# Turning the sums of an attention chunk with a 66-column fp32 product instead of 128-column transposes

## The chip, the cores and the metric

The kernel runs on one core of a Trainium2 chip. The metric is the device time of one execution in microseconds (us). The kernel before takes 3548.26 us, the median of 3 runs (3547.71 to 3548.54).

## What is computed

Two layers in sequence: differential attention over 2048 tokens of width 512 with 16 pairs of heads, a mixture of experts, a state-space layer and a quantised feed-forward layer, with a layer norm after each. The change lies in the attention alone:

```python
q = (x @ Wq).reshape(b, t, 2 * H, HD).transpose(0, 2, 1, 3) * scaling     # H = 16, HD = 16
k = (x @ Wk).reshape(b, t, 2 * H, HD).transpose(0, 2, 1, 3)
v = (x @ Wv).reshape(b, t, H, 2 * HD).transpose(0, 2, 1, 3)
scores = jnp.einsum('bhqd,bhkd->bhqk', q, k)
aw = jax.nn.softmax((scores + causal).astype(jnp.float32), axis=-1)
aw = aw.reshape(b, H, 2, t, t)
aw = aw[:, :, 0] - lam * aw[:, :, 1]
attn = jnp.einsum('bhqk,bhkd->bhqd', aw, v)
```

So each pair of heads has two softmaxes over the same keys, whose results are subtracted, and then multiplies with a V of 32 columns.

## The kernel before

The function `attention` works on 16 pairs (`p`), and in each on 4 chunks of 512 queries (`c`). A chunk has 4c + 4 key tiles of 128 keys, since later keys are hidden; one key tile of one chunk is a unit `u`, and a pair has 40. Scores are made turned, with keys on the partitions and queries along the row.

TensorE runs one program written out by hand (from L601). In each unit it does, in this order: `scores` for the unit two ahead (L560), products for the row maxima of a later pair (`max_scores`, L552), and `times_v` for this unit (L583). `times_v` multiplies the exponentials `PT` with `VS`, which holds V's 32 columns, a column of ones that gives the softmax's denominator, and zeros up to 64. The two softmaxes of a pair lie on partitions 0 to 63 and 64 to 127 of the sums `po`, so of its 128 rows 2 x 33 have a meaning: 0 to 32 and 64 to 96. Both products of a unit are full fp32.

At the end of a chunk ScalarE copies `po` to `OT` (L662). One unit later, after that unit's `times_v`, TensorE turns the copy with `turn_out` (L587 to L593): four transposes of 128x128, each giving 128 queries on the partitions and the 128 sums along the row. They fill one bank of PSUM, a slot of a ring of three that the products for the maxima use as well. VectorE's `combine` (L700 to L714) reads the slot: the reciprocals of the two denominators, their weights, two products with the 32 columns of each softmax, and the sum into `A`. It empties the slot with the last of these reads.

VectorE also takes the row maxima out of the ring (L681, L684), in the order in which TensorE fills it. Before TensorE writes a slot it waits until the tenant of three fillings ago is out (`await_ring`). ScalarE makes the exponentials (L628), copies the sums, and rounds weights for a later layer. GpSimd fills VS, stages V for each pair (L464), hides later keys in the diagonal units (L482), and takes the low parts of those weights. SyncE waits for the fills (L513) before it loads the third pair's queries and keys.

`g.ident` is the 128x128 identity in fp32, made at the start of the program.

Of the kernel before, what the change touches and what calls it, by code (L numbers as in the profile page):

```python
# [14 lines left out]
P = 128  # L15
# [12 lines left out]
VD = 2 * HD  # L28
# [318 lines left out]
def attention(nc, g, QD, KD, scan_w, next_w):  # L347
# [10 lines left out]
    MV = 64  # L358
# [58 lines left out]
    with ExitStack() as ctx:  # L417
        sb = lambda name, shape, dt=F32: ctx.enter_context(nc.sbuf_tensor(name, shape, dt))
# [4 lines left out]
        OT = [sb(f"outT{b}", [P, CHUNK]) for b in range(2)]  # L423
# [2 lines left out]
        mp = sb("neg_max_parts", [P, P], F32R)  # L426
        mT = sb("neg_max_turned", [P, P], F32R)
        rL = sb("inv_sums", [P, 4, 2])
        r2 = sb("weight2", [P, 4])
        o1, o2 = sb("out1", [P, 4, VD]), sb("out2", [P, 4, VD])  # L430
        w_raw = sb("w_raw", [P, 2, E])
# [4 lines left out]
        ring = [ctx.enter_context(nc.psum_tensor(f"ring{i}", [P, CHUNK], F32)) for i in range(RING)]  # L436
        pb = [ctx.enter_context(nc.psum_tensor(f"prob_scores{i}", [P, 2, CHUNK], F32)) for i in range(2)]
        po = ctx.enter_context(nc.psum_tensor("times_v", [P, CHUNK], F32))
        setup, mp_clear = g.sem("at_setup"), g.sem("max_parts_clear")
        loaded, max_in = [[g.sem(f"{n}{b}") for b in range(NQK)] for n in ("at_loaded", "at_max_in")]  # L440
        filled, emptied = g.sem("ring_filled"), g.sem("ring_emptied")
        max_all, max_high, max_low = (g.sem("max_" + n) for n in ("all", "high", "low"))
# [16 lines left out]
        with nc.Block() as block:  # L459

            @block.gpsimd
            def _(pool):
                def stage_v(p):
                    pool.tensor_copy(VS[p % 2][:, :, 0:VD], g.V[:, :, p * VD:(p + 1) * VD]).then_inc(v_staged, 1)  # L464

                for b in range(2):
                    pool.memset(VS[b][:, :, :], 0.0).then_inc(setup, 1)
                pool.wait_ge(setup, 2)
                for b in range(2):
                    pool.memset(VS[b][:, :, VD], 1.0).then_inc(setup, 1)  # L470
                stage_v(0)
                for b in range(2, NQK):
                    pool.memset(KS[b][:, :].bitcast(F32), 1.0).then_inc(setup, 1)
                pool.memset(mp[:, :].bitcast(F32), 0.0).then_inc(mp_clear, 1)
                for p in range(PAIRS):

                    if p:
                        stage_v(p)
                    for u in diag:
                        pool.wait_ge(exped, p * NU + u + 1)  # L480
                        keys = PT[u % NPT][:, :, 0:P]
                        pool.affine_select(out=keys, in_=keys, compare_op=ALU.is_ge, fill=0.0, base=0,  # L482
                                           pattern=[[0, 2], [1, P]], channel_multiplier=-1).then_inc(hidden, 1)
                        for n in range(by_unit.get(u, 0)):
                            k = len(SPLIT_AT) * p + n + (by_unit[11] if u > 11 else 0)
                            pool.wait_ge(w_high, k + 1)
                            if k >= 2:
                                pool.wait_ge(w_out[k % 2], 32 * (k // 2))
                            pool.tensor_tensor(w_lo[:, k % 2, :], w_raw[:, k % 2, :], w_hi[:, k % 2, :].bitcast(F32), ALU.subtract).then_inc(w_low, 1)  # L489
                        if p == PAIRS - 1 and u == ends[NCH - 2]:  # L490
                            for n in range(len(UP_AT)):
                                pool.wait_ge(up_high, n + 1)
                                pool.tensor_tensor(up_lo[:, piece(n)], g.raw_up[:, piece(n)], up_hi[:, piece(n)].bitcast(F32), ALU.subtract).then_inc(up_low, 1)
# [40 lines left out]
            @block.tensor  # L534
            def _(pe):
                def slot(n):
                    return ring[n % RING]

                def await_ring(n):

                    if n >= RING:
                        pe.wait_ge(emptied, n - RING + 1)

                def max_scores(q, t):
                    i, c = tiles[t]
                    w = tile_width(t)
                    if t == 0 and q > 1:
                        pe.wait_ge(loaded[q % NQK], loads(q))
                    await_ring(place["max", q, t, 1])
                    for s in range(2):  # L550
                        rows = slice(64 * s, 64 * s + PARTS)
                        pe.matmul(slot(place["max", q, t, s])[:, 0:w], QS[q % NQK][rows, i * P:(i + 1) * P],  # L552
                                  KS[q % NQK][rows, c * CHUNK:c * CHUNK + w], start=True, stop=True).then_inc(filled, 1)

                def scores(b, u):
                    c, j = units[u]
                    w = width(u)
                    for s in range(2):
                        rows = slice(64 * s, 64 * s + FULL)
                        mm = pe.matmul(pb[u % 2][:, s, 0:w], KS[b][rows, j * P:(j + 1) * P],  # L560
                                       QS[b][rows, (c + 1) * CHUNK - w:(c + 1) * CHUNK], start=True, stop=True)
                    mm.then_inc(scored, 1)

                def times_v(p, u):

                    c, j = units[u]
                    w = width(u)
                    if u in diag:
                        pe.wait_ge(hidden, p * ND + diag.index(u) + 1)
                    else:  # L570
                        pe.wait_ge(exped, p * NU + u + 1)
                    if u == 0:
                        pe.wait_ge(v_staged, p + 1)
                        if p == 0:
                            pe.wait_ge(setup, 4)
                    if j == 0:
                        if p or c:
                            pe.wait_ge(po_free, p * NCH + c)
                    halves = 2 if w > 256 else 1
                    h = w // halves  # L580
                    for n in range(halves):
                        for s in range(2):
                            mm = pe.matmul(po[MV * s:MV * (s + 1), CHUNK - w + n * h:CHUNK - w + (n + 1) * h], VS[p % 2][:, j, :],  # L583
                                           PT[u % NPT][:, s, n * h:(n + 1) * h], start=(j == 0 and n == 0), stop=(j == 4 * c + 3))
                    mm.then_inc(pt_free, 1)

                def turn_out(p, c):  # L587
                    n = place["out", p, c]
                    await_ring(n)
                    pe.wait_ge(po_free, p * NCH + c + 1)  # L590
                    for k in range(4):
                        mm = pe.transpose(slot(n)[:, k * P:(k + 1) * P], OT[c % 2][:, k * P:(k + 1) * P], g.ident[:, :])
                    mm.then_inc(filled, 1)  # L593

                def turn_maxima(q):
                    n = place["turn", q]
                    await_ring(n)
                    pe.wait_ge(max_low, q)
                    pe.transpose(slot(n)[:, 0:P], mp[:, :].bitcast(F32), g.ident[:, :]).then_inc(filled, 1)

                for u in range(LEAD):  # L601
                    scores(0, u)
                for p in range(PAIRS):
                    for u in range(NU):
                        n = p * NU + u
                        to = p + (u + LEAD) // NU
                        if to < PAIRS:
                            if u + LEAD == NU:
                                pe.wait_ge(max_in[to % NQK], rows(to))

                            pe.wait_ge(exped, n + 1)
                            scores(to % NQK, (u + LEAD) % NU)
                        for q, t in step_tiles(p, u):
                            max_scores(q, t)
                        if u == TURN_AT and p + 1 < PAIRS:
                            turn_maxima(p + 1)
                        times_v(p, u)
                        if u == 0 and p:
                            turn_out(p - 1, NCH - 1)
                        if u - 1 in ends:  # L620
                            turn_out(p, ends.index(u - 1))
                turn_out(PAIRS - 1, NCH - 1)

            @block.scalar
# [42 lines left out]
            def _(dve):  # L667
                def slot(n):
                    return ring[n % RING]
# [30 lines left out]
                def combine(p, c):  # L700
                    n, m = place["out", p, c], p * NCH + c
                    dve.wait_ge(filled, n + 1)
                    tp = slot(n)[:, :].rearrange("p (k s n) -> p k s n", k=4, s=2)
                    dve.reciprocal(rL[:, :, :], tp[:, :, :, VD]).then_inc(out_inv, 1)
                    dve.wait_ge(out_inv, m + 1)
                    dve.tensor_scalar(r2[:, :], rL[:, :, 1], g.neg_lam[:, :], None, ALU.mult).then_inc(out_weight, 1)
# [1800 lines left out]
```

## Time and profile before

| | before |
|---|---|
| median of 3 runs | 3548.26 us |
| the profiled execution | 3550.99 us, with a span of 3549.0 us from its first to its last instruction |
| TensorE matmul / weight load busy | 3370.3 us (95%) / 2378.6 us (67%) |
| VectorE / ScalarE / GpSimd busy | 2677.5 (75%) / 2110.0 (59%) / 880.6 us (25%) |
| mean granted clock of TensorE | 0.977 |
| attention, first to last instruction | about 166 to 1223 us |

"Busy" of TensorE counts the time in which any matmul is in flight. Matmuls are pipelined, so one that takes 0.27 us from start to end may follow the last after 0.11 us; what a step costs is read from starts, not from durations. Weight loads are listed as an engine of their own (PEld) and overlap the multiplies. In a row, `128*64 128x256` says that the array holds 128 rows and 64 columns of weights and that 256 columns stream through. `ring<-ident,outT` means that tile ring is written from ident (which streams) and outT (which is loaded as weights).

### The profile page before, as it was taken

What the parts mean: (1) busy time and instruction counts of PE and PEld (TensorE: products, weight loads), DVE (VectorE), ACT (ScalarE), POOL (GpSimd) and SP (SyncE); (2) the same over time, 40 slices, a digit from 0 to 9 for tenths busy, and PEclk for the clock granted to TensorE, in tenths of its full rate; (3) what the DMA queues carried; (4) which work ended last, traced back from release to release, by engine and by line L of the source; (5) the groups of instructions that cost most, each with busy time, mean ns of one, the idle gap of its engine ahead of it and who ended that gap; (6) DMA issues with size and microseconds to landing.
All of it is one profiled execution on the core that took longest, in us unless ns stands there. A gap on an engine that the chain in (4) does not pass through costs nothing. (4 is left out here: it accounts for less than half of the span.)

```text
span 3549.0 us, 58273 instructions
## 1 busy us (share of the span) xinstructions
PE 3370.3 (95%) x20672; PEld 2378.6 (67%) x20672; DVE 2677.5 (75%) x5224; ACT 2110.0 (59%) x3378; POOL 880.6 (25%) x818
## 2 busy tenths in 40 slices
PE   9899999999999888977999999999999999969998
PEld 7644444444444477765777777777777777758886
DVE  3577777777777484575999999999998999964444
ACT  3156666666667633434777777777777777743332
POOL 0012212222222300002344434443444444420000
PEclk9999999999999998988999999999999999989999
DMA  7333433433432211237666766677667766640100
GB/s 243 84 79 90 113 86 100 110 88 100 108 90 86 101 39 35 86 113 243 235 225 230 245 233 227 231 254 243 228 227 231 247 228 231 216 141 27 36 12 24
DMA packets 263840, 529.34 MB, mean 149 GB/s; under 512 B 32256, under 2 KB 54912, under 8 KB 260480
## 3 DMA queue, kind: packets, MB, share of 16 engines
q1 hardware_dynamic: 263552, 525.62, 46.7%
q8 instruction: 166, 2.72, 0.3%
q14 instruction: 122, 1.00, 0.1%
HBM read 429.55 MB, written 95.42 MB: 148 GB/s over the span
## 5 line engine op out<-in xcount | busy, mean ns | idle before, releaser
L628 ACT ACTIVATE probs<-prob_scores 128x1024 f32<-128x1024 f32 (+3 forms) x640 | 572.8, 897 | 382.2 <-PE prob_scores L560 374.4
L583 PE MATMUL times_v<-probs,VS 128*64 128x256 f32 (+2 forms) x4608 | 613.5, 382 | 17.5 <-ACT outT L662 12.7
L684 DVE TENSOR_REDUCE part_max<-ring 128x1 f32<-128x512 f32 x720 | 463.0, 686 | 112.4 <-PE ring L552 110.7
L49 PE MATMUL sc_pip<-sc_xh,sc_wl 128*128 128x512 f32 x1024 | 455.7, 445 | 22.3 <-DMA sc_xl<-x_low 15.4
L583 PEld LDWEIGHTS times_v<-probs,VS 128*64 128x64 f32 x4608 | 279.8, 136 | 256.8 <-issue 161.8
L51 PE MATMUL sc_pip<-sc_xh,sc_wh 128*128 128x512 f32 x1024 | 405.2, 396 | 0.0
L50 PE MATMUL sc_pip<-sc_xl,sc_wh 128*128 128x512 f32 x1024 | 403.9, 394 | 0.0
L1754 POOL TENSOR_TENSOR sc_xdd<-sc_xdt,sc_small 128x512 f32<-128x512 f32 x128 | 245.6, 1919 | 581.5 <-DVE sc_xdt L1965 581.5
L1890 ACT ACTIVATE sc_M<-sc_later,sc_small 128x128 f32<-128x128 f32 x1024 | 311.8, 390 | 0.0
L560 PE MATMUL prob_scores<-QS,KS 50*128 50x512 f32 (+3 forms) x1280 | 298.8, 464 | 4.0 <-ACT probs L628 2.1
L1956 DVE SCALAR_TENSOR_TENSOR sc_ca<-sc_xr,sc_chan,sc_ca 128x512 f32<-128x512 f32 x384 | 290.9, 758 | 13.6
L560 PEld LDWEIGHTS prob_scores<-QS,KS 50*128 50x128 f32 x1280 | 119.4, 183 | 217.2 <-ACT probs L628 119.1
L681 DVE CUSTOM_DVE_ANT_0 masked_scores<-ring,later_keys 128x128 f32<-128x128 f32 x480 | 216.4, 488 | 59.0 <-PE ring L552 56.4
L49 PEld LDWEIGHTS sc_pip<-sc_xh,sc_wl 128*128 128x128 f32 x1024 | 194.1, 190 | 96.8 <-issue 40.5
L552 PE MATMUL ring<-KS,QS 48*128 48x512 f32 (+3 forms) x1200 | 233.9, 386 | 14.3 <-DVE part_max L684 12.5
L50 PEld LDWEIGHTS sc_pip<-sc_xl,sc_wh 128*128 128x128 f32 x1024 | 194.3, 190 | 68.1 <-issue 29.5
L1774 POOL TENSOR_TENSOR sc_ssq<-sc_ssq,sc_sq 128x512 f32<-128x512 f32 x112 | 163.3, 1458 | 307.2 <-ACT sc_sq L1918 307.2
L51 PEld LDWEIGHTS sc_pip<-sc_xh,sc_wh 128*128 128x128 f32 x1024 | 193.5, 189 | 43.7
L1805 PE MATMUL sc_py<-sc_M,sc_xdt 128*64 128x128 f32 x2048 | 207.4, 281 | 10.2 <-DVE sc_M L1976 10.2
L2002 DVE TENSOR_TENSOR sc_gl<-sc_gx,sc_gh 128x512 fp32r<-128x512 f32 x128 | 216.4, 1690 | 0.0
L482 POOL TENSOR_SCALAR_AFFINE_SELECT probs<-probs 128x256 f32<-128x256 f32 x256 | 104.5, 409 | 449.2 <-ACT probs L628 449.2
L489 POOL TENSOR_TENSOR w_lo<-w_raw,w_hi 128x512 fp32r<-128x512 f32 x96 | 122.6, 1278 | 359.1 <-ACT w_hi L641 359.1
(376 smaller groups left out, 7163.6 us busy)
## 6 DMA issues: line engine op xcount, KB each, us to landing
sc_wh<-scan_W_high SPq DMA_DIRECT2D x256, 256.0 KB, 2.8
sc_wl<-scan_W_low SPq DMA_DIRECT2D x256, 256.0 KB, 3.4
sc_later<-scan_acum SPq DMA_DIRECT2D x128, 512.0 KB, 4.9
sc_ce<-scan_expa SPq DMA_DIRECT2D x128, 512.0 KB, 5.2
sc_woh<-scan_Wo_high SPq DMA_DIRECT2D x128, 256.0 KB, 4.1
sc_wol<-scan_Wo_low SPq DMA_DIRECT2D x128, 256.0 KB, 4.8
w_raw<-in_Wg SPq DMA_DIRECT2D x64, 256.0 KB, 2.9
scan_W_high<-w_hi SPq DMA_DIRECT2D x64, 256.0 KB, 2.0
```

Source lines behind the costliest of these rows:

```text
L49: pe.matmul(out, ll, rh, start=start, stop=False)
L50: pe.matmul(out, lh, rl, start=False, stop=False)
L51: return pe.matmul(out, lh, rh, start=False, stop=stop)
L552: pe.matmul(slot(place["max", q, t, s])[:, 0:w], QS[q % NQK][rows, i * P:(i + 1) * P], KS[q % NQK][rows, c * CHUNK:c * CHUNK + w], start=T ...
L560: mm = pe.matmul(pb[u % 2][:, s, 0:w], KS[b][rows, j * P:(j + 1) * P], QS[b][rows, (c + 1) * CHUNK - w:(c + 1) * CHUNK], start=True, stop= ...
L583: mm = pe.matmul(po[MV * s:MV * (s + 1), CHUNK - w + n * h:CHUNK - w + (n + 1) * h], VS[p % 2][:, j, :], PT[u % NPT][:, s, n * h:(n + 1) * ...
L628: act.activation(PT[u % NPT][:, :, 0:w], pb[u % 2][:, :, 0:w], ACT.Exp).then_inc(exped, 1)
L681: dve.tensor_tensor_reduce(out=masked_out[:, s, 0:w], in0=slot(n)[:, 0:w], in1=later[:, CHUNK - w:], scale=1.0, scalar=NEG, op0=ALU.add, o ...
L684: dve.tensor_reduce(to, slot(n)[:, 0:w], AX.X, ALU.max).then_inc(emptied, 1)
L1754: pool.tensor_tensor(xdd[t % 2][:, :, :], xdt[t % 2][:, :, :], bc(t, 1), ALU.mult).then_inc(xdd_made, 1)
L1890: act.activation(M[t % 2][:, h, :], later[t % 2][:, h, :], ACT.Relu, bias=small[b % 2][:, c, 3, h:h + 1], scale=-1.0).then_inc(relued, 1)
L1956: dve.scalar_tensor_tensor(out=to, in0=src, scalar=w, in1=to, op0=ALU.mult, op1=ALU.add).then_inc(conv if last else conv_step, 1)
```

## The change

A constant matrix `pick` of 128 x 66 is made of two copies of 33 columns of the identity: columns 0 to 32 and 64 to 96. `turn_out` multiplies by it, as an ordinary product in fp32, in place of each transpose. The four results lie side by side in 264 columns of the slot, and `combine` reads them there with another stride. GpSimd makes `pick` right after the first staging of V, ahead of the fills of the third K buffer and of the parts of the maxima, and TensorE waits for it once, at the first turned chunk.

```diff
         rL = sb("inv_sums", [P, 4, 2])
+
+        pick = sb("pick", [P, 2, VD + 1])
...
-        setup, mp_clear = g.sem("at_setup"), g.sem("max_parts_clear")
+        setup, mp_clear, picked = g.sem("at_setup"), g.sem("max_parts_clear"), g.sem("picked")
+        NP = 2 * (VD + 1)
...
                 stage_v(0)
+                for s in range(2):
+                    pool.tensor_copy(pick[:, s, :], g.ident[:, MV * s:MV * s + VD + 1]).then_inc(picked, 1)
...
                     pe.wait_ge(po_free, p * NCH + c + 1)
+                    if p == 0 and c == 0:
+                        pe.wait_ge(picked, 2)
                     for k in range(4):
-                        mm = pe.transpose(slot(n)[:, k * P:(k + 1) * P], OT[c % 2][:, k * P:(k + 1) * P], g.ident[:, :])
+                        mm = pe.matmul(slot(n)[:, k * NP:(k + 1) * NP], OT[c % 2][:, k * P:(k + 1) * P], pick[:, :, :], start=True, stop=True)
                     mm.then_inc(filled, 1)
...
-                    tp = slot(n)[:, :].rearrange("p (k s n) -> p k s n", k=4, s=2)
+                    tp = slot(n)[:, 0:4 * NP].rearrange("p (k s n) -> p k s n", k=4, s=2)
```

## Rows read from the trace of the kernel before

**Rows 1.** One stretch of attention: busy us of each engine, granted clock, DMA.
```profile
core 0: us, PE busy (x) PEld busy (x) DVE busy (x) ACT busy (x) POOL busy (x), PEclk, DMA share, GB/s
350.00:525.00 175.00, 171.21 (x1247) 85.33 (x1243) 135.22 (x369) 108.00 (x134) 39.96 (x63) 1.00 0.42 101
```

**Rows 2.** What TensorE waited for in attention: us in total, times, longest us.
```profile
PE times_v L583 <- ACT outT L662: 12.7, 47, 0.9
PE ring L552 <- DVE part_max L684: 12.5, 35, 0.8
PE times_v L583 <- POOL probs L482: 3.6, 2, 2.6
PE prob_scores L560 <- ACT probs L628: 1.2, 1, 1.2
PE ring L592 <- ACT outT L662: 0.8, 1, 0.8
```

**Rows 3.** The replaced line: duration min/median/max; then who waited for it.
```profile
L592 PEld LDWEIGHTS ring<-ident,outT x256: 137/141/231, 181.9 to 1220.8; 128*128 128x128 f32 x128
L592 PE MATMUL ring<-ident,outT x256: 272/273/476, 181.9 to 1220.9; 128*128 128x128 f32 x128
...
  DVE inv_sums L704: 92.1, 64
```

**Rows 4.** Timeline of one group: start us, length us, engine, line.
```profile
706.07 0.42 PEld L592 LDWEIGHTS ring<-ident,outT 128*128 128x128 f32 x4 [0.39 <-DVE part_max L681]
706.65 0.19 PEld L560 LDWEIGHTS prob_scores<-QS,KS 50*128 50x128 f32 x2 [0.17 <-issue]
...
706.07 0.66 PE L592 MATMUL ring<-ident,outT 128*128 128x128 f32 x4
```

**Rows 5.** Timeline: weight loads of four fp32 products of 128 columns each.
```profile
1580.10 0.97 PEld L1332 LDWEIGHTS ex_misc<-A 128*128 128x128 f32 x8
```

**Rows 6.** Two fp32 products of 256 columns: durations, and one group in time.
```profile
L1311 PE MATMUL ex_misc<-A x12: 378/381/634, 1462.0 to 1568.0; 128*128 128x256 f32 x12
...
1522.27 1.03 PE L1311 MATMUL ex_misc<-A 128*128 128x256 f32 x4
```

**Rows 7.** Timeline: weight loads for 136-column, then 512-column multiplies.
```profile
1290.60 0.19 PEld L49 LDWEIGHTS ao_pf<-ao_wf_high,rows_low 128*128 128x128 f32 x1
...
1291.83 0.19 PEld L51 LDWEIGHTS ao_pf<-ao_wf_high,rows_high 128*128 128x128 f32 x1
...
1292.05 0.19 PEld L50 LDWEIGHTS ao_po<-ao_wo_low,ao_ah 128*128 128x128 f32 x1
1292.29 0.19 PEld L51 LDWEIGHTS ao_po<-ao_wo_high,ao_ah 128*128 128x128 f32 x1
```

**Rows 8.** Timeline: weight loads of the first group in attention.
```profile
181.93 0.72 PEld L592 LDWEIGHTS ring<-ident,outT 128*128 128x128 f32 x4 [0.76 <-issue]
182.97 0.29 PEld L560 LDWEIGHTS prob_scores<-QS,KS 50*128 50x128 f32 x2 [0.33 <-issue]
```

**Rows 9.** Timeline of VectorE: the combine after the group of rows 4 begins.
```profile
706.76 0.21 DVE L704 RECIPROCAL inv_sums<-ring 128x8 f32<-128x8 f32 x1 [0.95 <-PE ring L592]
```

**Rows 10.** Timeline: TensorE's two waits after it, and the exp before a copy.
```profile
708.68 0.44 PE L552 MATMUL ring<-KS,QS 48*128 48x384 f32 x2 [0.19 <-DVE part_max L684]
...
711.83 1.08 PE L583 MATMUL times_v<-probs,VS 128*64 128x256 f32 x8 [0.19 <-ACT outT L662]
...
710.17 1.03 ACT L628 ACTIVATE probs<-prob_scores 128x1024 f32<-128x1024 f32 x1 [0.61 <-PE prob_scores L560]
```

**Rows 11.** Timeline at the start of attention: GpSimd, then TensorE.
```profile
167.99 0.17 POOL L470 MEMSET VS<- 128x16 f32 x2
168.09 0.61 POOL L464 COPY VS<-V_then_X 128x512 f32<-128x512 f32 x1
...
170.53 0.77 POOL L482 TENSOR_SCALAR_AFFINE_SELECT probs<-probs 128x256 f32<-128x256 f32 x2
...
171.00 0.69 PE L583 MATMUL times_v<-probs,VS 128*64 128x256 f32 x2 [2.56 <-POOL probs L482]
```

## What the change should do to the time, worked out beforehand

> **What bounds the kernel now.** I read the table by stretches first [rows 1]. The changed lines run only inside attention, and the row there says what fills it: in 350 to 525 us TensorE has a matmul in flight for 171.21 us of 175, VectorE is busy 135.22, ScalarE 108.00, GpSimd 39.96, and the granted clock is 1.00, the 2.4 GHz level. The stretches up to 1050 look the same. A TensorE that is busy 98% is not by itself the bound, because matmul spans overlap, so I read the list of what TensorE waited for in all of attention next [rows 2]: 12.7 us for the copy of the sums, 12.5 us for VectorE to empty a ring slot, 3.6 for GpSimd, 1.2 and 0.8 for two more, and one line under that, together about 31 us of 1050. TensorE sets the pace, and what is added to its stream is added to the time unless one of these waits gives it back.
>
> The line that the change replaces is read in [rows 3]: 256 transposes in 64 groups of four. VectorE waited for them 64 times of 64 (92.1 us): it is always idle when a group ends. The single group at 706 us [rows 4] is the measure of today's cost. Its first weight load starts at 706.07, the first load of the next step (scores) at 706.65: a group holds TensorE for 0.59 us, rounding up. Nearly all of the 64 are alike: of the 256 multiplies the shortest takes 272 ns and the middle one 273 [rows 3]. It divides like this: four multiplies span 0.66 us of which the last takes 0.27, so they start (0.66 - 0.27)/3 or, without the longer first one, 0.109 apart; the last starts at 706.46, its columns need another 0.11, to 706.57, and the next load starts 0.09 later, in the change from one array shape to another.
>
> **What replaces it.** A product in full fp32 is two weight loads and two multiplies in this kernel, not one: the source line of the products with A has 8 of each for 4 calls [rows 5]. So a chunk goes from 4 loads and 4 multiplies of 128 columns to 8 loads and 8 multiplies of 66.
>
> The multiply. Four of 256 fp32 columns span 1.03 us and one is 0.38, so they follow each other by 0.216 [rows 6]; that is 0.84 ns a column, and 66 columns are 0.056 us. Eight make 0.45 us, about what four transposes take now (4 x 0.109 = 0.44). By columns alone the change is worth nothing: 8 x 66 = 528 of them against 4 x 128 = 512.
>
> The weight load. The stationary operand is still 128 columns of the copied sums. A transpose loads it in 0.14 us [rows 3], a load for an fp32 product takes 0.19 [rows 5], so the latter holds the load path some 0.05 longer. How close such loads can follow is shown by the rows that are nearest to the new code [rows 7]: twelve loads of 128x128 for multiplies of 136 columns at one pass (a multiply there is as short as the new one: loads for 512 such columns follow at 0.24, at 1292.05 and 1292.29, so 136 columns are 0.064 us). First at 1290.60, twelfth at 1291.83: 1.23/11 = 0.112 us apart, although the multiplies need only half of that. The loads set the pace and the multiplies hide behind them. In [rows 5], with 128 fp32 columns, eight loads span 0.97 us with 0.19 the last: (0.97 - 0.19)/7 = 0.111. Two places, the same 0.11.
>
> Speaking against the change by another way is the Trainium skill, "TensorE: Matmul & The Clock Gate", section "LDWEIGHTS (loading the stationary operand)": a load takes as many ns as it has columns divided by 1.2, whatever the rows, which would be 107 ns each and +0.42 us a chunk, or +27 us in all; [rows 5, 7] agree within 5 ns, though the transposes' own loads [rows 3] are shorter than that rule lets them be. The same page, section "Back-to-back issue gap", has pairs of load and multiply at 128 columns about 81 ns apart; what that would give is the fourth rival.
>
> **The sum for one chunk**, from first load to the next step's first load: 7 gaps of 0.1115 = 0.78; the eighth load 0.11; its multiply's columns 0.056; the change of array shape 0.09. Together 1.04 us against 0.59: +0.45 us. The shape change stays because the new product uses the same 128 by 128 shape as the transpose. Bounds: 0.107 (a bare 128 columns at the rate of [rows 6], 128 x 0.84 ns) to 0.118 a gap gives +0.42 to +0.50.
>
> 62 chunks run at full clock, and the last one too, though its end is followed by the end of attention: there VectorE was idle for long and the combine follows at once, so its 0.45 is on the path as well. 63 x 0.45 = 28.4 us. The first chunk, at 181.93 us, runs at half the rate (0.72 for the four loads against 0.42, next load after 1.04 us) [rows 8]: the 0.95 of loads and columns doubles to 1.89, plus 0.1, so about 2.0, +0.95 us. TensorE: **+29.3 us**, bounds 27 to 32.
>
> **Does a wait give it back?** The nearest wait after a group is the one for a ring slot. VectorE's combine takes the slot after the group and cannot start before it; at 706.76 VectorE has been idle 0.95 us when it does [rows 9]. TensorE then waits 0.19 us at 708.68 for a slot [rows 10]. Both sides of this wait count from the end of the group (combine on one side, scores, maxima product and times-V on the other), so a group that ends 0.45 later moves both, and the wait stays. The other wait is times-V of a new chunk for ScalarE's copy of the last (0.19 at 711.83): ScalarE had been idle 0.61 before the exp ahead of that copy, waiting for TensorE's scores, so this too counts from TensorE. Nothing gives back by these two samples; the bound is all 31 us of [rows 2], and I take 0. Below nothing there is no place: VectorE's five operations of the combine read the same 8 and 128 elements, now from 264 packed columns instead of 512; the nearest rows (0.21 to 0.29 us each) show no dependence that could be measured, and VectorE isn't the pace anyway. If its slack were gone, the price would be the group's delay again, no more.
>
> **GpSimd and the waits.** Two copies of 33 columns are put behind the first staging of V. That queue is on the path at one place: the first mask (170.53) releases TensorE's first times-V after 2.56 us of idling [rows 11]. A copy of 512 columns takes 0.61 us, two memsets of 16 together 0.17, so the two cost between 0.1 and 0.6; by size they are nearest to the small ones, and I take **+0.2 us**. Queued behind them are also the fill of the third K buffer, for which SyncE waits before loading pair 2, and the clearing of the parts of the maxima, needed by VectorE: both are wanted only after unit 33 of pair 0, some 50 us later, so these cost nothing. TensorE's new wait for the copies stands at 181.93, 12 us after they are made; behind it are the product and all later work, and it costs nothing either. No DMA is added. The added buffer is 264 bytes a partition and moves nothing.
>
> **Total: +29.5 us.** The profiled execution took 3550.99 us with a span of 3549.0; it would become 3580.5. It lies 2.7 above the median of 3548.26, which would become **3577.8 us** (+0.83%).
>
> **The rivals.**
> 1. The loads don't set the pace: either they load as quickly as the transposes' (0.14 instead of 0.19, a gap of 0.055), or a product of ones and zeros is issued in one load and not in two, which is also the way in which the change might not do what it says. Then a chunk is 0.05 + 8 x 0.056 + 0.09 = 0.59, as now, and the kernel takes 3548.5: not slower. It decides from the point where a load's gap is under the 0.056 of its multiply. For it: the columns are equal, and today's loads are quick. Against it: every fp32 or split product of 128 weight columns in the trace loads in 0.19 with 0.11 between, and the products of [rows 5] come in twos. 8%.
> 2. Loads and multiplies don't overlap when the multiply is this short: 8 x (0.11 + 0.056) + 0.09 = 1.42, +0.83 a chunk, 3602. Against it are the multiplies of 136 columns [rows 7], but these stream in one pass and mine in two. 5%.
> 3. Part of it is given back in the waits for a slot and for the copied sums. They are 25.2 us in all; half of that would give 3565. Against it stands what was said of both samples. 7%.
> 4. The loads keep closer than the rows at hand: +13 us, 3562. The mechanism would be that a load runs ahead by more than one multiply and shares its path; eight pairs at 0.08 are 0.65, plus 0.06 and 0.09, +0.21 a chunk. The skill's figure of about 81 ns named above would give just this. [rows 7] measure pairs of nearly that size at 0.112 and speak against it. 4%.
>
> **How the numbers follow.** The forecast has 76%: 3577.8, with its own bounds (27 to 32 and 0.1 to 0.6, against the median) of 3575 to 3581. The range of 8 in 10 is 3564 to 3582: the forecast and the third rival. About 0.2%, or 7 us, is what a measurement here can tell from none: slower has the forecast, rivals 2, 3 and 4 but for a bit of the third (0.91); same has the first (0.07); faster 0.02, for what the first might bring below zero.
>
> **What would show it.** In the changed kernel's trace: 512 loads and 512 multiplies at the replaced line, loads of 0.19; eight loads spanning 0.97; from a group's first load to the next step's first load 1.04; the waits of [rows 2] the same within 2 us; the first times-V at 171.2; attention ending 29 to 30 us later, and every later stretch of the same length. Wrong would make it: loads of 0.14, a group of 0.6 or of 1.4, or a wait of VectorE or ScalarE that has shrunk by some tens of per cent.

## The result, and the profile after

| | before | after |
|---|---|---|
| median, same chip | 3547.99 us (4 runs) | 3581.11 us (4 runs, 3576.61 to 3582.02) |
| ratio | 1 | 1.0093, 95% interval 1.0075 to 1.0110 |
| profiled execution / its span | 3550.99 / 3549.0 us | 3580.65 / 3578.8 us |
| groups of one chunk, first load to the next step's first load | 0.59 us | 1.04 us |
| attention, first scores to the next stage's first transpose | 166.13 to 1225.96: 1059.8 us | 167.41 to 1253.57: 1086.2 us |

The change makes the kernel slower by 33 us in the medians and by 29.8 us between the two profiled executions. 26.3 of these 29.8 us lie in attention. The other 3.5 lie before it (1.3) and after it (2.2), in stages of which no line was changed. Such stretches moved by more than that between other profiles: with the same measure, the runs below have 165.1 to 167.1 us ahead of attention and 2317 to 2331 us behind it. Nothing here ties them to the change.

The replaced line in the kernel after, which answers [rows 3] (duration min/median/max in ns, forms, who waited), and TensorE's waits in attention, which answer [rows 2]:

```profile
L599 PEld LDWEIGHTS ring<-pick,outT x512: 185/192/193, 181.8 to 1248.5; 128*128 128x128 f32 x171
L599 PE MATMUL ring<-pick,outT x512: 274/275/326, 181.8 to 1248.5; 128*128 128x66 f32 x171
...
  DVE inv_sums L711: 122.5, 64
```
```profile
PE times_v L588 <- ACT outT L669: 12.8, 47, 0.9
PE ring L557 <- DVE part_max L691: 9.7, 24, 0.8
PE times_v L588 <- POOL probs L487: 3.1, 1, 3.1
PE prob_scores L565 <- ACT probs L635: 1.8, 1, 1.8
PE ring L599 <- ACT outT L669: 0.8, 1, 0.8
PE prob_scores L565 <- DMA QS<-neg_max_turned: 0.6, 2, 0.4
```

There are 512 weight loads of 0.19 us in place of 256 of 0.14, and VectorE waits 30 us longer in all for the same 64 groups (122.5 against 92.1). The wait for ring slots has fallen from 12.5 us in 35 places to 9.7 in 24: something was given back. One group in time, against [rows 4], and the same group of the next pair (start, length, engine, line):

```profile
716.09 0.97 PEld L599 LDWEIGHTS ring<-pick,outT 128*128 128x128 f32 x8 [0.38 <-DVE part_max L688]
717.13 0.18 PEld L565 LDWEIGHTS prob_scores<-QS,KS 50*128 50x128 f32 x2
...
782.87 0.97 PEld L599 LDWEIGHTS ring<-pick,outT 128*128 128x128 f32 x8 [0.38 <-DVE part_max L688]
```

717.13 - 716.09 = 1.04, and the eight loads start (0.97 - 0.19)/7 = 0.111 apart. The two groups are 782.87 - 716.09 = 66.78 us apart. In the kernel before the same two are at 706.07 [rows 4] and

```profile
771.47 0.42 PEld L592 LDWEIGHTS ring<-ident,outT 128*128 128x128 f32 x4 [0.38 <-DVE part_max L681]
```

which is 65.40 apart. Four groups lie in that stretch and should add 4 x 0.45 = 1.80 us; they add 1.38. So each group costs what was forecast, and 0.4 us a pair comes back somewhere.

**Where it comes back.** Going through the starts of times-V (its first weight load) unit by unit, in pairs 1 to 14 the two kernels differ by +0.45 at each of the four groups, by +0.31 and +0.45 at unit 38 of pairs 6 and 11, and at one unit of every pair: unit 26, the second after the third chunk's group. There the kernel after is 0.45 us faster in pairs 0 to 10, and 0.21 slower in pairs 11 to 14. Pair 5, whose rows follow, is at this place like every pair from 1 to 10. First the kernel before: VectorE's combine, GpSimd's subtraction of weight parts, and TensorE's product for the maxima in unit 26.

```profile
549.60 0.21 DVE L704 RECIPROCAL inv_sums<-ring 128x8 f32<-128x8 f32 x1 [1.12 <-PE ring L592]
549.84 0.72 DVE L706 TENSOR_SCALAR weight<-inv_sums,neg_lam 128x4 f32<-128x4 f32 x1
550.48 0.28 DVE L707 TENSOR_TENSOR out<-ring,inv_sums 128x128 f32<-128x128 f32 x1
...
549.26 1.28 POOL L489 TENSOR_TENSOR w_lo<-w_raw,w_hi 128x512 fp32r<-128x512 f32 x1 [4.93 <-ACT w_hi L641]
...
552.01 0.50 PE L552 MATMUL ring<-KS,QS 48*128 48x512 f32 x2 [0.33 <-DVE part_max L684]
```

The second operation works on 4 elements a partition and takes 0.72 us, where the middle one of 64 takes 0.229. It starts inside the subtraction, which ends at 549.26 + 1.28 = 550.54, and ends with it, at 550.56. The slot is emptied half a microsecond late, VectorE gets to the next maxima late, and TensorE waits 0.33 us. The kernel after, same pair and place:

```profile
557.01 0.21 DVE L711 RECIPROCAL inv_sums<-ring 128x8 f32<-128x8 f32 x1 [1.59 <-PE ring L599]
557.25 0.26 DVE L713 TENSOR_SCALAR weight<-inv_sums,neg_lam 128x4 f32<-128x4 f32 x1
...
556.22 1.27 POOL L494 TENSOR_TENSOR w_lo<-w_raw,w_hi 128x512 fp32r<-128x512 f32 x1 [4.92 <-ACT w_hi L648]
...
558.96 0.50 PE L557 MATMUL ring<-KS,QS 48*128 48x512 f32 x2
```

The combine now starts 0.79 us after the subtraction instead of 0.34, because its group ended 0.45 later, while the subtraction did not move: in both kernels it starts 4.15 us after the times-V of unit 22. The small operation now starts 0.24 us before the subtraction ends and takes 0.26, and TensorE doesn't wait. In pairs 11 to 14 ScalarE scales the weights before it rounds them, so the subtraction comes later, and the combine runs into it from its start (pair 12):

```profile
1026.11 1.02 DVE L713 TENSOR_SCALAR weight<-inv_sums,neg_lam 128x4 f32<-128x4 f32 x1
...
1025.83 1.28 POOL L494 TENSOR_TENSOR w_lo<-w_raw,w_hi 128x512 fp32r<-128x512 f32 x1 [5.69 <-ACT w_hi L648]
...
1028.57 0.50 PE L557 MATMUL ring<-KS,QS 48*128 48x512 f32 x2 [0.63 <-DVE part_max L691]
```

Here the small operation takes 1.02 us and TensorE's wait is 0.63. The Trainium skill has a rule for this in "SBUF — State Buffer", section "SBUF: two separate sides": VectorE and GpSimd share a pair of ports as an exclusive lock, which the one that starts first keeps for its whole instruction. VectorE takes part in it with operations in a two-port mode, or with two inputs from SBUF against a GpSimd operation that reads SBUF. The rows agree: the small operation has two inputs in SBUF (`inv_sums` and `neg_lam`), and its end and the subtraction's coincide to 0.02 us, while the reciprocal, which reads the ring in PSUM, kept its 0.21 us inside the subtraction (at 549.60). That the subtraction is the cause is tested below by moving it; that the ports are the way in which it acts rests on the skill and on these rows.

### The profile page after: what moved, and what is told of

It is laid out like the page before. It is cut to its first block and busy times, and to the rows that moved or that the text cites. A ratio compares the mean times of both kernels' runs of the same rounds, so it can differ in the third digit from the quotient of the medians.

```text
span 3578.8 us, 58787 instructions
## 1 busy us (share of the span) xinstructions
PE 3403.4 (95%) x20928; PEld 2418.9 (68%) x20928; DVE 2673.1 (75%) x5224; ACT 2109.0 (59%) x3378; POOL 881.1 (25%) x820
## 5 line engine op out<-in xcount | busy, mean ns | idle before, releaser
L588 PE MATMUL times_v<-probs,VS 128*64 128x256 f32 (+2 forms) x4608 | 614.8, 383 | 17.1 <-ACT outT L669 12.8
L50 PEld LDWEIGHTS sc_pip<-sc_xl,sc_wh 128*128 128x128 f32 x1024 | 194.6, 190 | 67.7 <-issue 29.1
L494 POOL TENSOR_TENSOR w_lo<-w_raw,w_hi 128x512 fp32r<-128x512 f32 x96 | 122.5, 1276 | 372.1 <-ACT w_hi L648 372.1
```

What stands on the lines that cost most here:

```text
L50: pe.matmul(out, lh, rl, start=False, stop=False)
```

## The experiments

Each was timed beside the kernel before on the same chip; ratios are against it. "Unit 26" is the time between the starts of times-V of units 25 and 26.

**x1_copies: GpSimd's copies alone.** The changed kernel with the transposes, and `combine`'s stride with them, put back:

```diff
-                        mm = pe.matmul(slot(n)[:, k * NP:(k + 1) * NP], OT[c % 2][:, k * P:(k + 1) * P], pick[:, :, :], start=True, stop=True)
+                        mm = pe.transpose(slot(n)[:, k * P:(k + 1) * P], OT[c % 2][:, k * P:(k + 1) * P], g.ident[:, :])
```

> The changed kernel's two GpSimd copies of 33 columns and TensorE's wait for them, but the four transposes as before. Theory: the copies stand ahead of the first mask and cost what they took in the changed kernel's trace (0.36 us, with 0.3 to the next start), once: +0.3 us, groups of 0.59 us as before, and TensorE's waits in attention as before (12.7 us for the copied sums, 12.5 for ring slots). Rival: the copies or the new wait shift something that lasts, and part of the +33 us of the change is theirs: over +2 us.

3550.48 us against 3549.11, ratio 1.0005 (0.9995 to 1.0015): not told apart from nothing, and over 2 us isn't excluded by the times alone. The trace has the groups at 0.59 and the waits as before (12.8 and 12.7 us). The two copies together span 0.36 us and hold the next fill for 0.30 (changed kernel):

```profile
169.92 0.36 POOL L476 COPY pick<-ident 128x33 f32<-128x33 f32 x2
170.22 1.80 POOL L478 MEMSET KS<- 128x2048 f32 x1
```

**x2_all128: the fp32 product with all 128 columns**, and `combine`'s stride to match.

```diff
-                        mm = pe.matmul(slot(n)[:, k * NP:(k + 1) * NP], OT[c % 2][:, k * P:(k + 1) * P], pick[:, :, :], start=True, stop=True)
+                        mm = pe.matmul(slot(n)[:, k * P:(k + 1) * P], OT[c % 2][:, k * P:(k + 1) * P], g.ident[:, :], start=True, stop=True)
```

> The fp32 product as in the change, but with all 128 columns of the identity in place of the 66. Theory (eight weight loads set the pace at 0.1115 us each and the multiplies hide behind them): only the last multiply is longer, 0.107 in place of 0.056, so a group takes 1.09 us where the changed kernel's took 1.037, +3.3 us over the changed kernel, about 3584. Rival (the streamed columns set the pace, or add to the loads): each multiply's 0.05 more is paid, 8 x 0.05 = 0.41 a group, +26 us over the changed kernel, about 3607.

Loads in time:

```profile
721.05 0.97 PEld L599 LDWEIGHTS ring<-ident,outT 128*128 128x128 f32 x8 [0.39 <-DVE part_max L688]
722.14 0.19 PEld L565 LDWEIGHTS prob_scores<-QS,KS 50*128 50x128 f32 x2
```

A group takes 1.09 us: nearly twice the columns cost 0.05. The rival's 1.45 is out. The kernel before goes further the other way, in a later stage: fp32 products with multiplies of a single column, here seven weight loads of one such group, at a granted clock of 1.00:

```profile
L2163 PE MATMUL fi_ring<-fi_ones,fi_ssq x32: 164/250/352, 3155.5 to 3356.8; 128*128 128x1 f32 x32
...
3265.08 0.86 PEld L2163 LDWEIGHTS fi_ring<-fi_ones,fi_ssq 128*128 128x128 f32 x7
```

They start (0.86 - 0.19)/6 = 0.112 apart. With 1, 66 and 128 columns the spacing is the same 0.111 to 0.112, so the columns don't set it. The loads do, or a fixed spacing of such pairs of load and multiply, which no run here tells from the loads. The time was 3579.1, ratio 1.0079 (1.0064 to 1.0094), where 3584 was expected. The two kernels were not timed side by side, and 3 us is less than runs of one kernel scatter, so the expected +3.3 shows in the groups only. The 66 columns save next to nothing against 128.

**x3_onepass: half the loads.** The sums and the matrix as fp32r, so that a product is one load and one multiply (the low bits of the sums are left out):

```diff
-        OT = [sb(f"outT{b}", [P, CHUNK]) for b in range(2)]
+        OT = [sb(f"outT{b}", [P, CHUNK], F32R) for b in range(2)]
...
-        pick = sb("pick", [P, 2, VD + 1])
+        pick = sb("pick", [P, 2, VD + 1], F32R)
```

> The change with the copied sums and the matrix rounded to fp32r: a product is then one weight load and one multiply, both of the sizes of the change, so this halves the count of loads (the sums lose low bits by it). Theory (loads of 128 columns 0.1115 us apart set the pace): 3 x 0.1115 + 0.11 for the fourth load + 0.03 of columns + 0.09 for the change of array shape = 0.56 us a group, 0.02 to 0.03 under the kernel before, whose time it matches within 3 us. Rival (streamed columns set the pace): 4 x 0.03 + 0.05 + 0.09 = 0.26 a group, 21 us under the kernel before.

```profile
704.14 0.52 PEld L599 LDWEIGHTS ring<-pick,outT 128*128 128x128 f32 x4 [0.39 <-DVE part_max L688]
704.71 0.19 PEld L565 LDWEIGHTS prob_scores<-QS,KS 50*128 50x128 f32 x2
```

0.57 us a group (0.564 in the middle of the 64), as the loads give, and not the 0.26 of the columns. 3551.48 us, ratio 1.0003 (0.9993 to 1.0014): the time of before. This halves loads and multiplies together; since x2 has ruled out the columns, the doubled number of load-and-multiply pairs is the whole cost of the change, and the shortened stream has no value while such a pair takes 0.11.

**x7_rows97: the columns cut in the transposes.** The kernel before, with transposes of partitions 0 to 96:

```diff
-                        mm = pe.transpose(slot(n)[:, k * P:(k + 1) * P], OT[c % 2][:, k * P:(k + 1) * P], g.ident[:, :])
+                        mm = pe.transpose(slot(n)[:, k * P:k * P + MV + VD + 1], OT[c % 2][0:MV + VD + 1, k * P:(k + 1) * P], g.ident[0:MV + VD + 1, 0:MV + VD + 1])
```

> The kernel before with transposes of the first 97 partitions alone (0 to 96, which hold all 66 rows with a meaning), so that 97 columns stream in place of 128 and the loads stay the transposes' quick ones. Theory: a transposed column streams in 0.84 ns and the load (about 0.055) is under it, so four transposes follow at 0.083 in place of 0.109: 0.49 us a group in place of 0.587, 64 x 0.10 = 6.4 us less, unless VectorE's combine, now earlier by 0.1, lies further into GpSimd's subtraction at unit 26 (up to 0.1 us in 15 pairs, 1.5 us back): about 3543. Rival: transposes are bound by their loads or a fixed spacing and the group stays at 0.587: the time of before.

```profile
705.70 0.37 PEld L592 LDWEIGHTS ring<-ident,outT 97*128 97x128 f32 x4 [0.38 <-DVE part_max L681]
706.18 0.19 PEld L560 LDWEIGHTS prob_scores<-QS,KS 50*128 50x128 f32 x2
```

0.48 us a group, 0.10 less. The edit cuts the rows of each load (128 to 97) along with the columns that stream, and no run parts the two; the loads kept their length (141 ns), the multiplies went from 273 to 247 ns. Unit 26 went from 2.28 to 2.38 and from 2.37 to 2.47: an earlier combine lies further in the subtraction, so the third group's 0.10 is lost, as was allowed for. 3546.53 us against 3548.99, ratio 0.9988 (0.9979 to 0.9996): faster, by 2.5 us in the medians and 4 by the ratio, where 5 were expected.

**x5_before_shift and x6_after_shift: the subtraction later, on both kernels.**

```diff
-    SPLIT_AT = (15, 17, 26, 28, 30, 32)
+    SPLIT_AT = (15, 17, 28, 30, 32, 34)
```

> The kernel before, with ScalarE's four weight roundings of a pair's second half moved two units later (28, 30, 32, 34 in place of 26, 28, 30, 32), so that GpSimd's subtraction for the first of them no longer lies beside the combine of the third chunk. Theory: in the kernel before that subtraction holds up a VectorE operation of this combine until it ends (0.72 us where 0.23 is usual), and TensorE waits 0.33 to 0.42 us more for a ring slot at unit 26 of 15 pairs. Without it: TensorE's wait for ring slots falls from 12.5 to about 7 us, unit 26 has no wait over 0.2, and the time falls by 4 to 6 us, to about 3543. Rival: the long VectorE operation is chance or comes from PSUM, the wait at unit 26 stays, within 1 us of before.

> The changed kernel with the same move of the four weight roundings. Theory: with the collision out of both kernels the change costs its groups' full 64 x 0.45 = 28.8 us and 0.3 for the copies, nothing given back: 29 us more than the shifted kernel before of this call. Pair by pair TensorE is 1.80 us later, where change against before showed 1.38 to 1.40 in pairs 1 to 10 and 2.04 to 2.06 in pairs 12 to 14. Rival: the give-back belongs to the later group itself (VectorE's longer rest), and pairs 1 to 10 still show about 1.4.

Unit 26 is 1.78 to 1.80 us in every pair from 1 to 14 of both, and pairs 2 to 8 differ by 1.75 to 1.84 us. So the give-back belongs to the collision and not to the group. The time went the other way than expected for the kernel before: 3554.62 us, ratio 1.0012 (1.0003 to 1.0022). The other took 3586.17, ratio 1.0098 (1.0073 to 1.0123), 32 us more where 29 were expected. The waits of x5_before_shift say why it lost:

```profile
PE ring L552 <- DVE part_max L684: 7.3, 20, 0.8
PE times_v L583 <- POOL probs L482: 6.8, 2, 3.9
PE ring L552 <- DVE part_max L681: 3.2, 10, 0.5
PE prob_scores L560 <- DMA QS<-neg_max_turned: 3.2, 4, 1.4
```

The first line fell from 12.5 as expected. The others are new or larger: SyncE stores the weight parts ahead of loading the turned maxima, so later roundings make these late, and the last pair ends behind GpSimd. A move of the rounding moves a whole queue.

**x9_rows97_early and x10_after_early: the first of the four roundings at unit 24**, `SPLIT_AT = (15, 17, 24, 28, 30, 32)`, on the kernel of 97 partitions and on the changed one.

> The kernel of 97 partitions with ScalarE's rounding of unit 26 done at unit 24, so that GpSimd's subtraction is over before the third chunk's combine. Theory: unit 26 falls from 2.28 to 1.78 us in pairs 0 to 10 and from 2.37 to 1.78 in pairs 11 to 14, as it did when that rounding came later: 5.5 + 2.4 = 7.9 us less on top of the 97 partitions' 6.4, about 3535. Rival: the rounding at unit 24 makes the copy of the sums late (it stands two exps ahead of it) and what is won at unit 26 is lost in the first times-V of the last chunk: TensorE's wait for the copied sums rises from 12.8 us by several us.

> The changed kernel with the same rounding at unit 24. Theory: its collision in pairs 11 to 14 goes (2.58 to 1.78 us at unit 26, 3.2 us), the one in pairs 0 to 10 was gone already (1.82): about 3 us less than the changed kernel, 3577 where that took 3581, and pair by pair 1.80 us plus 0.10 x 4 longer than the kernel of 97 partitions with the same move (2.20 us). Rival: as in the kernel of 97 partitions, the copy of the sums becomes late.

3548.03, ratio 1.0000 (0.9990 to 1.0011), where 3535 was expected, and 3593.6, ratio 1.0127 (1.0110 to 1.0144). Unit 26 fell as the theory said, to 1.78 to 1.80 but in the few pairs with a fallen clock, and most pairs of the two kernels are 2.20 us apart, but the rival ate it up: TensorE's wait for the copied sums rose from 12.7 to 19.5 us in both. Unit 24 rose from 1.47 to 1.66 us and to 2.41 in pairs 11 to 14, since the copy of the sums stands behind the rounding:

```profile
999.01 0.71 ACT L637 ACTIVATE w_raw<-w_raw,w_norm 128x512 f32<-128x512 f32 x1
999.75 0.63 ACT L641 ACTIVATE w_hi<-w_raw 128x512 fp32r<-128x512 f32 x1
1000.29 1.01 ACT L628 ACTIVATE probs<-prob_scores 128x1024 f32<-128x1024 f32 x1
1001.19 0.59 ACT L662 ACTIVATE outT<-times_v 128x512 f32<-128x512 f32 x1
...
1001.92 1.08 PE L583 MATMUL times_v<-probs,VS 128*64 128x256 f32 x8 [1.19 <-ACT outT L662]
```

The changed kernel also lost about 9 us in pairs 11 and 12 (73.9 and 70.6 us where others take 67.7), where TensorE's granted clock was 0.79 in 960 to 985 us and 0.91 in 1000 to 1040; I expected 3577, which was wrong by 17.

**x14_before_wait, x13_after_wait, x12_rows97_wait: only GpSimd waits.** ScalarE's order stays, and the one subtraction is held until the combine is over:

```diff
                             pool.wait_ge(w_high, k + 1)
+                            if u == 23 and n == 0:
+                                pool.wait_ge(exped, p * NU + 28)
```

> The kernel before, in which GpSimd waits for the exp of unit 27 before its first subtraction of a pair's second half, so that this one stands behind the third chunk's combine; ScalarE's order is untouched, and the other three subtractions stay. Theory: unit 26 falls from 2.28 and 2.37 to 1.78 us, unit 24 stays at 1.47 (it rose to 1.66 and 2.41 where the rounding itself came earlier), so a pair takes 64.9 us in place of 65.4 and attention 7 to 8 us less; about 3541. Rival: the delayed subtraction makes the weights' stores and loads late, and TensorE waits for turned maxima or ScalarE for weights by as much.

> The changed kernel with the same wait of GpSimd. Theory: its pairs 1 to 10 stay at 66.7 to 66.8 us, since their unit 26 was free of the collision (1.82, now 1.78), and pairs 11 to 14 lose 0.8 each (2.58 to 1.78). Against the kernel before with the same wait each pair is 1.80 us longer and the whole 28 to 30 us, as the groups' 0.45 alone give; the give-back of 0.4 a pair is gone. Rival: pairs stay 1.4 apart, and the give-back has another cause.

> The kernel of 97 partitions with the same wait of GpSimd: both gains at once. Theory: groups of 0.484, unit 26 at 1.78 in place of 2.38 and 2.47 (0.60 x 11 + 0.69 x 4 = 9.4 us), pairs of 64.5 us in place of 65.1; about 3537, some 12 us under the kernel before. Rival: as for the kernel before with this wait.

The small operation of the combine, in this order of kernels (the changed kernel had a maximum of 1031 ns, the kernel before 724):

```profile
L708 DVE TENSOR_SCALAR weight<-inv_sums,neg_lam x64: 229/229/231, 183.6 to 1216.4; 128x4 f32<-128x4 f32 x64
```
```profile
L715 DVE TENSOR_SCALAR weight<-inv_sums,neg_lam x64: 229/229/231, 186.0 to 1250.8; 128x4 f32<-128x4 f32 x64
```
```profile
L708 DVE TENSOR_SCALAR weight<-inv_sums,neg_lam x64: 229/229/231, 181.5 to 1206.4; 128x4 f32<-128x4 f32 x64
```

No instance is stretched any more; in x14 and x13 nothing but the subtraction was moved. Unit 26 is 1.77 to 1.79 us in all three, in pairs 1 to 14. Two groups one pair apart, in the kernel before with the wait and in the changed kernel with it:

```profile
703.47 0.42 PEld L594 LDWEIGHTS ring<-ident,outT 128*128 128x128 f32 x4 [0.38 <-DVE part_max L683]
...
768.40 0.42 PEld L594 LDWEIGHTS ring<-ident,outT 128*128 128x128 f32 x4 [0.39 <-DVE part_max L683]
```
```profile
722.71 0.97 PEld L601 LDWEIGHTS ring<-pick,outT 128*128 128x128 f32 x8 [0.39 <-DVE part_max L690]
...
789.45 0.97 PEld L601 LDWEIGHTS ring<-pick,outT 128*128 128x128 f32 x8 [0.39 <-DVE part_max L690]
```

64.93 and 66.74 us: 1.81 apart, the 4 x 0.45 in full, with nothing given back. The times: 3543.22, ratio 0.9989 (0.9979 to 0.9998), for the kernel before with the wait; 3582.04, ratio 1.0089 (1.0073 to 1.0104), for the changed one; and **3538.62, ratio 0.9974 (0.9965 to 0.9983)** for 97 partitions with the wait, which is 9 to 10 us faster than the kernel before and 44 faster than the changed one. The first lies 2 us above the 3541 expected, the last 2 above 3537. The first two are 38.8 us apart in the medians, and some 35 by the ratios, where 28 to 30 were expected. Of the 43 us between their profiles 25 lie in pairs 1 to 14, as the groups give; the rest lies in pair 0 (4.8), in pair 15 (3.2) and outside attention (9.9, of which 8.6 behind it). No run here explains that rest. Outside attention x12 and x14, the same in all those stages, also lie 9.2 us apart.

**x15_after_again: the changed kernel once more.**

> The changed kernel itself, for a second profile and more times beside these. Theory: groups of 1.037, unit 26 at 1.82 and 2.58 and pairs of 66.77 and 67.5 come back to 0.02 us, since they are the program's; the later than usual end of pair 15 (3.35, 1.74 and 2.52 us in units 33 to 35, where the first profile's clock fell) need not, and without it attention is 2 to 3 us shorter. Rival: it comes back in full and belongs to the change's price.

3582.8, ratio 1.0093 (1.0079 to 1.0107). Groups, unit 26 (1.82, and 2.58 to 2.60) and pairs of 66.75 and 67.5 us came back. Units 34 and 35 of pair 15 took 1.45 and 1.39 in place of 1.74 and 2.52, so the fallen clock there is not part of the change's price; unit 33 took 3.17, against 2.71 in the kernel before and 2.26 in x1, and its cause was not looked for. Attention was not shorter for it, though: pair 0 took 82.9 us where the first profile had 74.7.

## Why the prediction was right

- **The time.** 3577.8 was forecast in a range of 3564 to 3582; 3581.11 was measured, near the upper end. The medians moved by 33.1 us and, in the repetition x15, by 34.3, against +29.5; between the profiled executions it was +29.8.
- **The count of instructions, the pace of the loads, the sum of a group.** 512 loads of 0.19, 0.111 apart, 1.04 us a group: as forecast; x2 varies the columns alone, and x3 the number of load-and-multiply pairs. The first rival (columns as pace, a group of 0.59) and the second (no overlap of short multiplies, 1.42) are out, by the 1.04 us itself and by the 1.09 and 0.57 of x2 and x3.
- **The fourth rival, and the figure of 81 ns in the Trainium skill** ("TensorE: Matmul & The Clock Gate", section "Back-to-back issue gap"). Pairs of load and multiply at these sizes were 111 ns apart in the change and 112 in [rows 7].
- **An aside with the wrong rows.** The prediction reads from [rows 3] that the transposes' loads are shorter than 107 ns each would let them be. The 0.14 us there is longer. What shows it is how close they follow: 0.093 apart on average in [rows 4], (0.42 - 0.14)/3, and 0.08 in x7, (0.37 - 0.14)/3, with the same 128 columns loaded. Nothing in the sum hung on it.
- **Nothing given back: wrong.** The third rival was partly true, at another place than it named a mechanism for. The step that failed is the reasoning from two samples of waits [rows 10]. Both samples do move with the group, and their kind still waits as before (12.8 us for the copied sums). But the combine has a third party, GpSimd, whose subtraction doesn't move with the group, and that shows only at the third chunk. I had looked at the combine of one fourth chunk (0.95 us of idle time before it, [rows 9]) and took it for all four. It gave back 11 x 0.45 = 4.9 us and took 4 x 0.21 = 0.8.
- **The first group: wrong in detail.** It was expected at the lower clock, 2.0 us, and ran at the full one in the first profile (1.04) and at 1.9 in x15's. That is a matter of the single execution.
- **The copies: right.** +0.2 us was taken and 0.30 measured. The waits of unit 38 for the turned maxima's load (0.6 us in two pairs) were not foreseen; x15 has them again in the same pairs.
- **The sum came out so near by luck in part.** In attention, 63 x 0.45 = 28.4, less 4.9, plus 0.8, plus 0.8 at unit 38 of two pairs, plus 2.6 in pair 15, less some 1.4 for a quicker pair 0 gives 26.3. The overestimate of 3 us in attention was made up by 3.5 us outside it, which the prediction had as nil. That is a matter of these two executions; in the medians the change costs 4 to 5 us more than forecast, which is within their intervals (27 to 39 us, and 28 to 38 in x15). Where the collision is out of both kernels each pair costs the forecast's own sum, 1.8 us.

## What to carry to other kernels

Count weight loads before columns: an fp32 product of 128 weight columns is here two loads 0.11 us apart, and until its multiplies stream for longer than that, fewer columns buy nothing, while a transpose of the same tile is one load and one multiply. Cutting the transpose by its input partitions instead, from 128 to 97, did save time: 0.10 us a group. And when a step moves in time, look at every place at which it recurs and at engines that don't move with it: a GpSimd operation of 1.3 us beside a VectorE operation on 4 elements cost TensorE 0.5 us a pair, more than the neighbouring waits that I had read.

## What the runs showed that I had not expected

- A VectorE operation whose operands are all in SBUF, started during a GpSimd subtraction over SBUF, ended with it to 0.02 us (it took up to 724 and 1031 ns instead of 229). Its neighbours of the same combine that read PSUM kept their length. Pair 12 of the kernel before shows both: the product of 0.28 us lies wholly inside the subtraction, and the last operation, all in SBUF, is the one caught (0.88 us where 0.29 is usual; 1008.40 + 0.88 = 1009.28, 0.15 us after GpSimd's 1007.85 + 1.28 = 1009.13):

```profile
1008.02 0.28 DVE L710 TENSOR_TENSOR out<-ring,weight 128x128 f32<-128x128 f32 x1
1008.40 0.88 DVE L714 TENSOR_TENSOR A<-out 128x128 f32<-128x128 f32 x1
...
1007.85 1.28 POOL L489 TENSOR_TENSOR w_lo<-w_raw,w_hi 128x512 fp32r<-128x512 f32 x1 [5.68 <-ACT w_hi L641]
```

- The start of attention varies more than the effects looked at. TensorE's granted clock over 166 to 260 us was 0.96 in the changed kernel's first profile and 0.85 in its second, and pair 0 took 74.7 and 82.9 us. The other profiles fit in: at a clock of 0.96 there pair 0 took 73 to 75 us, whichever the kernel, and at 0.89 78 to 80. Whether the change makes the low clock last longer there is open: of the kernels with eight loads a group pair 0 took 74.7 to 82.9 us, of those with four 73.2 to 78.5. The lines for the two profiles of the same kernel (busy us of the engines, then granted clock, DMA share, GB/s):

```profile
166.00:260.00 94.00, 82.52 (x583) 42.59 (x583) 65.49 (x187) 48.88 (x62) 20.93 (x37) 0.96 0.42 91
```
```profile
166.00:260.00 94.00, 84.01 (x535) 42.48 (x535) 59.63 (x170) 44.49 (x56) 20.91 (x36) 0.85 0.38 86
```
